# A decoder layer on one core: first and last stage cut by sequence

## The reference, cut to what matters

```python
x = x + self_attn(layernorm(x))          # causal, 16 query heads, 4 key heads of 16, rotary positions
x = x + cross_attn(layernorm(x), ctx)    # 16 heads, an integer mask of 256 x 256, the same for all
x = x + ffn(layernorm(x))                # 256 -> 1024 -> relu -> 256, hidden values and w2 rounded to 8 bits

q = rope((h @ Wqa @ Wqb).reshape(b, s, 16, 16))     # low-rank queries
kv = (h @ Wkva @ Wkvb).reshape(b, s, 4, 16, 2)      # low-rank keys and values; k = rope(kv[..., 0])
```

## Time and profile before

| | us |
|---|---|
| median of 3 runs | 1891.46 (1891.41 to 1894.48) |
| the profiled execution | 1879.75 |
| its span | 1878.1 |
| busy in the span: PE | 1683.7 (90%) |
| DVE | 1242.5 (66%) |
| ACT | 1110.7 (59%) |
| POOL | 701.0 (37%) |

### The profile page before, as it was taken

How to read it: one execution, slowest core, us unless ns; L and a number is a source line. 1 busy time by engine, 2 the same in 40 slices (tenths; PEclk the granted TensorE clock), 3 DMA queues, 4 the chain that set the end, 5 groups by cost and what they waited for, 6 DMA issues and landing times.

```text
span 1878.1 us, 34264 instructions
## 1 busy us (share of the span) xinstructions
PE 1683.7 (90%) x12302; PEld 1017.6 (54%) x12302; DVE 1242.5 (66%) x1908; ACT 1110.7 (59%) x1720; POOL 701.0 (37%) x962
## 2 busy tenths in 40 slices
PE   2879989899998989999899999989999898999887
PEld 1445555556554655655556554655655555565554
DVE  4467576676857667575776857668585766857562
ACT  3355665756567465656756566475656746565563
POOL 3260533625144261533526153262524426152300
PEclk7879999999999999999999998999999999999999
DMA  6351632725254270633626163271625427063310
GB/s 173 51 89 26 94 66 37 121 26 86 47 80 78 35 124 8 87 64 52 106 35 94 31 93 65 35 124 20 89 50 74 84 35 111 18 88 55 51 31 12
DMA packets 86607, 124.09 MB, mean 66 GB/s; under 512 B 10481, under 2 KB 53938, under 8 KB 86322
## 3 DMA queue, kind: packets, MB, share of 16 engines
q1 hardware_dynamic: 83650, 115.26, 40.5%
q0 software_dynamic: 2160, 7.87, 1.1%
q10 hardware_dynamic: 768, 0.57, 0.1%
HBM read 21.42 MB, written 8.39 MB: 16 GB/s over the span
## 4 chain that ended last, share of the span: by engine, by line
PE 62%; POOL 9%; issue 9%; ACT 7%; DMA 7%; DVE 6%; SPq 1%; POOLq 0%; ACTq 0%
PE o_pair L1312 12%; PE small L1398 7%; PE score L1273 6%; PE small L1429 5%; PE small L1143 4%; DMA Q<-q2p 3%; PE small L1325 3%; DVE negmax L894 3%; PE score L1250 3%; DMA Q<-negT 2%; PE score L1231 2%; PE score L1196 2%; PE small L1159 2%; POOL x L494 2%; POOL q1f L518 2%
## 5 line engine op out<-in xcount | busy, mean ns | idle before, releaser
L689 ACT ACTIVATE P<-score 128x1024 f32<-128x1024 f32 x448 | 448.4, 1025 | 145.5 <-PE score L1250 56.6
L894 DVE TENSOR_REDUCE negmax<-score 128x4 f32<-128x1024 f32 (+1 forms) x384 | 463.3, 1221 | 66.4 <-PE score L1231 49.9
L916 DVE TENSOR_TENSOR P<-P,cross_bound 128x1024 f32<-128x1024 f32 x192 | 251.0, 1330 | 118.1 <-ACT P L689 118.1
L1312 PE MATMUL o_pair<-P,V 128*32 128x256 f32 (+1 forms) x4096 | 293.8, 374 | 0.3 <-DVE P L916 0.3
L465 POOL TENSOR_TENSOR negrest<-negmax,negparts 128x32 f32<-128x32 f32 x64 | 15.9, 248 | 629.9 <-ACT negparts L650 629.5
L735 ACT ACTIVATE score<-cross_q 128x1024 f32<-128x1024 bf16 x192 | 194.9, 1021 | 31.8 <-DVE negmax L894 31.1
L1429 PE MATMUL small<-xnT,w 128*128 128x256 f32 x720 | 185.2, 379 | 0.0
L1273 PE MATMUL score<-Q,K 99*128 99x256 bf16 x1024 | 168.1, 291 | 8.2 <-ACT P L689 4.3
L1312 PEld LDWEIGHTS o_pair<-P,V 128*32 128x32 f32 x4096 | 87.3, 109 | 142.7 <-issue 86.7
L1231 PE MATMUL score<-K,Q 96*128 96x256 bf16 x768 | 119.3, 279 | 40.1 <-ACT score L735 19.7
L1273 PEld LDWEIGHTS score<-Q,K 99*128 99x128 bf16 x1024 | 87.4, 102 | 112.4 <-issue 63.6
(11 more groups left out here) (181 smaller groups left out, 3142.1 us busy)
## 6 DMA issues: line engine op xcount, KB each, us to landing
Q<-q1p SPq DMA_DIRECT2D x96, 256.0 KB, 5.9
K<-k2p SPq DMA_DIRECT2D x96, 256.0 KB, 8.3
Q<-q2p SPq DMA_DIRECT2D x192, 128.0 KB, 4.5
x_in<-in_x SPq DMA_DIRECT2D x16, 512.0 KB, 5.6
ctxT<-in_ctx SPq DMA_DIRECT2D x16, 512.0 KB, 6.3
k2f<-q1f SPq DMA_DIRECT2D x32, 256.0 KB, 4.9
out_y<-x POOLq DMA_DIRECT2D x15, 512.0 KB, 6.1
K<-k1p SPq DMA_DIRECT2D x96, 64.0 KB, 4.5
```

What stands on the lines that cost most here:

```text
L689: A.activation(P[:, t % 4, :], score[b][:, :, :], ACT.Exp, scale=SCALE).then_inc(score_free[b], 1)
L894: V.tensor_reduce(negmax[:, k, h:h + 1024 // w], s.rearrange("p (h w) -> p h w", w=w), AX.X, ALU.max, negate=True).then_inc(score_free[b], 1)
L916: V.tensor_tensor(p, p, cross_bound[:, t % 2, :].unsqueeze(1).broadcast_to([128, 4, SEQ]), ALU.min).then_inc(probs_masked[1], 1)
L1312: last = T.matmul(o_ps[ob][32 * j:32 * j + 32, SEQ * gg + q0:SEQ * gg + SEQ], v, p, start=s == 0, stop=end, tile_position=(0, 32 * j), ski ...
```

## The change

The first stage. SP loads the mask, `b2` and `w2` right after the eight small weights and ahead of `ctxT` and the twelve others, each with a semaphore of its own. DVE prepares the mask and rounds `w2` and `b2` ahead of the rotation. The rotation and the cut into parts of the queries go by sequence (256 of the 512 tokens of each of two feature tiles), first sequence first; the keys' rotation, rest and third part move from POOL to DVE, between those of the queries. The query transfers are halved: 2 x 6 of 128 KB, all for the first sequence ahead of those for the second. The six key transfers are issued from POOL's queue. ACT writes the ones of `K2` in two pieces, ahead of its first copy and behind the values, and those of `K1` last. PE starts on the scores of the first sequence when its queries and the keys are there, waits for `loaded` only ahead of `key2`, and waits for the second sequence's queries ahead of tile 6. The transposes of the mask no longer wait for `loaded`.

The end stage. The first sequence's attention output is turned inside `attend`, after tile 15 of the shifted scores and ahead of the last three products with V. `out2_0` comes ahead of the last unit's turn. Residual, norm sums, inverse root, norm, turn (`xnT3_0`, `xnT3_1`), hidden tiles and output go by sequence: `h0_0` to `h0_3` are the hidden tiles of the first sequence (two tiles of 256 tokens to a bank), then `xnT3_1`, `ffn0`, `h1_0` to `h1_3`, `ffn1`. On DVE the last unit's `normalise` stands behind the norm's sums of the first sequence.

```diff
-END_USERS = over(2, ["m2T_1", "o2t0", "o2t1", "o2t2", "oT2_0", "o2t3", "out2_0", "oT2_1", "out2_1", "xnT3_0",
-                     "xnT3_1"] + [f"h{t}" for t in range(HT)] + ["ffn0", "ffn1"])
+END_USERS = over(2, ["m2T_1", "o2t0", "o2t1", "oT2_0", "o2t2", "out2_0", "o2t3", "oT2_1", "xnT3_0", "out2_1"]
+                 + [f"h0_{j}" for j in range(HT // 2)] + ["xnT3_1", "ffn0"] + [f"h1_{j}" for j in range(HT // 2)]
+                 + ["ffn1"])
...
 @block.sync
+            def put_queries(n, b, done):
+                at = slice(SEQ * b, SEQ * b + SEQ)
+                for t, p in enumerate(Q_PART):
+                    if p == n:
+                        sp.dma_start(Q1[HD * t:HD * t + HD, :, at].rearrange("d (h c) t -> d h c t", c=NC),
+                                     q1p[:, n, :, at]).then_inc(done, 16)
...
             sp.wait_ge(loaded_self, 16 * LOADS_SELF)
+            sp.dma_start(mask[:, :, :], d["mask"]).then_inc(loaded_mask, 16)
+            sp.dma_start(b2[:, :], d["b2"]).then_inc(loaded_w2, 16)
+            sp.dma_start(w2[:, :, :], d["w2"]).then_inc(loaded_w2, 16)
             sp.dma_start(ctxT[:, :, :], ctx_v[0]).then_inc(ctx_loaded, 16)
...
             swap_pairs(PRO)
             for n in range(3):
-                put_part("k1", n, 0)
-                put_part("q1", n, 0)
+                sp.wait_ge(first_q1, (4, 6, 7)[n])
+                put_queries(n, 0, stacked_first)
+            for n in range(3):
+                sp.wait_ge((part1, part2, part3)[n]["q1"], 1)
+                put_queries(n, 1, stacked["q1"])
...
 @block.gpsimd
-            rope_products("k1", cosk, sink, k1s, 0)
-            rope_sum("k1", k1s, 0)
-            rest("k1", 0)
-            third("k1", 0)
+            for n in range(3):
+                pool.wait_ge((part1, part2, part3)[n]["k1"], 1)
+                for t, p in enumerate(K_PART):
+                    if p == n:
+                        pool.dma_start(K1[HD * t:HD * t + HD], k1p[:, n, :]).then_inc(stacked_first_k1, 16)
...
-            inverse_root(2, NG - 1)
+            for b in range(GB):
+                pool.wait_ge(ln_step[2], LN_STEPS * (NG + b))
+                at = slice(2 * b, 2 * b + 2)
+                G.tensor_tensor(rstd[2][:, at], vareps[2][:, at], minus_half[:, at], ALU.pow).then_inc(rstd_ready[2], 1)
...
 @block.scalar
             A.activation(carrier[:, 0:1], minus_half[:, 0:1], ACT.Exp)
+            ones(K2[KROWS:SROWS, 0:HEADS // 2, :])
             turns(PRO, "xnT1_", inT)
...
             values1(PRO)
+            ones(K2[KROWS:SROWS, HEADS // 2:HEADS, :])
+            first_part(0)
             part("k1", 0, whole, part1, 0)
-            part("q1", 0, whole, part1, 0)
+            first_part(1)
             part("k1", 1, rest1, part2, 0)
-            part("q1", 1, rest1, part2, 0)
-            for t in (K1, K2):
-                A.activation(t[KROWS:SROWS, :, :], ...)
+            second_part(0)
+            second_part(1)
+            ones(K1[KROWS:SROWS, :, :])
...
+            turn_batch(END, "oT2_1", 1, inT)
+            turn_batch(END, "xnT3_0", 0, xnT3)
+            hidden_half(0)
+            turn_batch(END, "xnT3_1", 1, xnT3)
+            ffn_out(END, 0)
+            hidden_half(1)
+            ffn_out(END, 1)
...
 @block.vector
+            product(q[0], cosq, first_q1)
+            product(other[0], sinq, first_q1)
+            dve.wait_ge(swapped["k1"], 32)
+            product(k, cosk, cosine["k1"])
+            product(other_k, sink, sine["k1"])
+            dve.wait_ge(first_q1, 2)
+            summed(q[0], other[0], first_q1)
+            ...
+            summed(k, other_k, whole["k1"])
+            product(q[1], cosq, cosine["q1"])
+            dve.wait_ge(first_q1, 4)
+            V.tensor_tensor(q[0], q[0], q1p[:, 0, :, 0:SEQ], ALU.subtract).then_inc(first_q1, 1)
+            dve.wait_ge(part1["k1"], 1)
+            V.tensor_tensor(k1f[:, :], k1f[:, :], k1p[:, 0, :], ALU.subtract).then_inc(rest1["k1"], 1)
+            product(other[1], sinq, sine["q1"])
+            dve.wait_ge(first_q1, 6)
+            V.tensor_tensor(q1p[:, 2, :, 0:SEQ], q[0], q1p[:, 1, :, 0:SEQ], ALU.subtract).then_inc(first_q1, 1)
+            dve.wait_ge(part2["k1"], 1)
+            V.tensor_tensor(k1p[:, 2, :], k1f[:, :], k1p[:, 1, :], ALU.subtract).then_inc(part3["k1"], 1)
+            ...
+            summed(q[1], other[1], whole["q1"])
             bk = PRO.bank("maskT")
...
+            normalise(END, 1, 2, NG - 1)
+            for b in range(GB):
+                at = range(2 * b, 2 * b + 2)
+                residual(END, "out2", b, x3, x2)
+                residual_done(END, "out2", b)
+                norm_stats(2, x3, NG - 1 + b, at, at)
+                if b == 0:
+                    normalise(END, 1, 3, NG - 1)
+                norm_apply(2, x3, NG - 1 + b, at)
...
 @block.tensor
                 else:
-                    pe.wait_ge(stacked["q1"], 16 * TERMS * (i + 1))
-                    pe.wait_ge(stacked["k1"], 16 * TERMS * (i + 1))
+                    pe.wait_ge(stacked_first, 16 * TERMS)
+                    pe.wait_ge(stacked_first_k1, 16 * TERMS)
                     self_scores(i, [0, 1])
                 self_scores(i, [2])
                 if not prev:
+                    pe.wait_ge(loaded, 16 * LOADS)
                     pe.wait_ge(ctx_loaded, 16 * (i + 1))
                     key2(st, 0)
...
+                if not prev:
+                    pe.wait_ge(stacked["q1"], 16 * TERMS)
                 self_scores(i, [6])
...
+            batch_copied(END, "oT2_0")
+            tokens(END, "out2", inT, wo2, 0)
+            unit_turn(END, 1, NG - 1, 3)
+            for u in range(2, UNITS):
+                pe.wait_ge(small_free[END.bank(f"o2t{u}")], END.this(f"o2t{u}"))
+            turned_batch(END, "oT2_1", 1, o)
+            pe.wait_ge(xn_ready[2], NG)
+            turned_batch(END, "xnT3_0", 0, xn)
+            batch_copied(END, "oT2_1")
+            tokens(END, "out2", inT, wo2, 1)
+            batch_copied(END, "xnT3_0")
+            hidden_half(0)
+            pe.wait_ge(xn_ready[2], NG + 1)
+            turned_batch(END, "xnT3_1", 1, xn)
+            ffn_ready(0)
+            ffn_out(END, 0)
+            batch_copied(END, "xnT3_1")
+            hidden_half(1)
+            ffn_ready(1)
+            ffn_out(END, 1)
```

More of the change, by code:

```diff
@@ L702, in exponentials @@
                     turn_batch(st, "oT1_0", 0, oT)
+                if last:
+                    turn_batch(st, "oT2_0", 0, inT)
                 unit_out(UNITS - 1)
@@ L838, in _, with hidden_half @@
             cut_first(1, NG - 1, 1)
[L839 to L849, removed]
+            exponentials(END, 1, NG - 1, last=True)
+            def hidden_half(b):
+                for j in range(HT // 2):
+                    bk = END.bank(f"h{b}_{j}")
+                    act.wait_ge(small_full[bk], END.this(f"h{b}_{j}"))
+                    bank, free = small[bk], small_free[bk]
+                    A.activation(carrier[:, j:j + 1], minus_half[:, 0:1], ACT.Copy)
+                    for n in range(2):
+                        t = 2 * j + n
+                        last = A.activation(hq[:, t, SEQ * b:SEQ * b + SEQ], bank[:, SEQ * n:SEQ * n + SEQ], ACT.Relu,
+                                            bias=b1[:, t:t + 1], saturate=False)
+                    last.then_inc(free, 1)
+            turn_batch(END, "oT2_1", 1, inT)
[5 more added lines that the diff above has]
+            ffn_out(END, 1)
         @block.vector
@@ L1378, in attend @@
                         times_v(st, a, g, t - LAG)
+                    if at_end == "last" and t == n:
+                        for u in range(2):
+                            pe.wait_ge(small_free[st.bank(f"o2t{u}")], st.this(f"o2t{u}"))
+                        turned_batch(st, "oT2_0", 0, o)
                     u = (t - LAG - 2) // TPU[a] - 1
@@ L1461, in _ @@
                 value1(PRO, r)
-            pe.wait_ge(loaded, 16 * LOADS)
             bk = PRO.bank("maskT")
@@ L1593, in _ @@
-            pe.wait_ge(small_free[END.bank("oT2_1")], END.this("oT2_1"))
-            tokens(END, "out2", inT, wo2, 1)
-            pe.wait_ge(xn_ready[2], NG)
-            for c in range(NC):
-                turned(END, f"xnT3_{c}", xn, c)
-            copied(END, "xnT3_")
-            hidden(END, range(HT))
-            pe.wait_ge(small_free[END.bank(f"h{HT - 1}")], END.this(f"h{HT - 1}"))
-            for r in range(2):
-                ffn_out(END, r)
+            attend(END, 1, NG - 1, "last")
@@ new lines, in hidden_half @@
+            def hidden_half(b):
+                at = slice(SEQ * b, SEQ * b + SEQ)
+                for j in range(HT // 2):
+                    bk = END.bank(f"h{b}_{j}")
+                    pe.wait_ge(small_free[bk], END.before(f"h{b}_{j}"))
+                    bank, filled = small[bk], small_full[bk]
+                    for n in range(2):
+                        t = 2 * j + n
+                        for c in range(NC):
```

(9 more changed lines are left out.)

93 lines of the change are left out of this document (38 added, 55 removed).

## The result

The changed kernel takes 1873.18 us (median of 8 runs, 1869.71 to 1879.8), the kernel before 1891.02 (8 runs, 1881.7 to 1894.48). The ratio is 0.992, 95% interval 0.9897 to 0.9943: 10.8 to 19.5 us faster. 1876.5 was predicted, with a range of 1867 to 1887. Timed again beside other runs of before, it gave 0.9918 (0.9897 to 0.9938), 15.0 us between the medians.

What follows compares the result with a forecast made beforehand. TensorE bounds the untouched loop; the gain lies where PE stands still at both ends. Start 11 us plus end 4 us give 15: 1891.46 - 15 = 1876.5 us, range 1867 to 1887.

Steps and rivals of the forecast that it cites:

- The swap: First stage: the swapped queries land at 24.5 us as before, since the same bytes are loaded.
- DVE's steps: First stage, rotation on DVE: 0.62 us a step, 1.14 at most; five steps end at 27.65.
- POOL's issues: First stage, six key transfers issued from POOL: 0.86 us each at first, the last ending at 34.1.
- Rival B: First stage: POOL's issues are slow, first score at 44.4, kernel 1882 us; chance 0.09.
- "earliest": First score's early limit: POOL's last issue plus its stores' quickest landing, 34.1 + 3.4 = 37.5 us.
- The rate: First stage transfers: 1.18 MB needed by the first score at 129 GB/s take 9.1 us.
- Behind the first score: Second sequence's queries through at 44.9, tile 6 due at 49.7: covered by 4.8 us.
- The end: End stage by sequence, fewer PE waits: 4 us gained, between 1 and 6.
- "the cost is as before": End stage: if the clock falls behind PE's pause, it costs some 2.8 us as before; gain about 3.
- The difference of 11.7 us: Whole kernel: the median's excess over the profiled time before, carried over unchanged to the forecast.
- "a mean group over 112.5 us": Loop: a mean group time above 112.5 us would show the forecast wrong.
- rival D: Loop falls in otherwise: slow groups more often, 1889 us, or less often, 1866; chance 0.13, of which 0.08 slow.

Runs made afterwards that it cites:

- all queries first: Changed kernel, but the first score also waits for the second sequence's query transfers; 1881.26 us, run once under the profiler.
- small loads first: Changed kernel with the six small or short-rowed of the twelve other weights loaded ahead of the six large ones; 1880.97 us, run once under the profiler.

## Why the prediction was right, step by step

**The swap** was to be unchanged at 24.5. It was 26.05, the late landing just told. That is the 1.5 us by which this profile's gain of 9.15 falls short of 11.0; over the interval the gain is 25.71 - 15.05 = 10.66, and 10.1 to 10.9 in six further profiles of kernels with this start (15.64 with the keys on SP, 14.77 to 15.16 in the others).

**DVE's steps** were taken as 0.62 us. The rows from 26 to 35:

```profile
26.66 0.69 DVE L1038 TENSOR_TENSOR k2f<-k2f,sinq 128x512 f32<-128x512 f32 x1
27.27 0.68 DVE L1038 TENSOR_TENSOR k1f<-k1f,cosk 64x512 f32<-64x512 f32 x1
...
33.29 0.68 DVE L1043 TENSOR_TENSOR q1f<-q1f,k2f 128x512 f32<-128x512 f32 x1
...
34.82 2.87 DVE L1081 TENSOR_TENSOR q1f<-q1f,q1p 128x512 f32<-128x512 f32 x1
38.39 0.69 DVE L1083 TENSOR_TENSOR q1p<-q1f,q1p 128x512 bf16<-128x512 f32 x1 [0.70 <-ACT q1p L805]
```

From start to start it is 0.60 (26.05, 26.66, 27.27), for 64 partitions as for 128. SP's first issue came at 29.84; that is the predicted 28.3 moved by the 1.5 us of the swap. The prediction said that POOL had no arithmetic there any more. It has, and a later paragraph of the prediction names it: its sum of `x_in` (34.38 to 37.13) lies beside the second half's rest, which took 2.87 us instead of 0.68. That step failed, and cost nothing: it is off the path, and it only sets why SP's twelve issues take 10.46 us with gaps, why `x_in` is issued at 40.41 and not 38, and, in the kernel that waits for all the queries, the 2.81 us in the chain above. The Trainium skill, SBUF — State Buffer, "SBUF: two separate sides", says that a VectorE operation with two SBUF inputs and a GpSimd operation that reads SBUF exclude each other on a shared port pair; the trace agrees: 2.87 us beside POOL's 2.75 us, and 0.67 us for the same operation in the kernel with the keys on SP, where POOL was idle.

**POOL's issues** were to cost 0.86 us and end at 34.1. They took 3.26 us for six and ended at 34.38: 0.71 for the first, about 0.5 each for the others, though they begin 2.2 us later, at 31.11 (1.5 from the swap, 0.64 between the semaphore and the issue). Rival B, slow issues, did not come. The last key transfer landed 7.1 us behind its issue, not in the 3.4 us of the prediction's "earliest" case: there was a backlog, as the byte rate wanted it.

**The rate.** 129 GB/s was taken from the kernel before, 141 measured: 1.41 MB in the ten us. A packet of the query halves took 29 ns in the first us (318 packets, 57% of the engines from 31 to 32) and 72 ns with the engines full (528 packets, 118% from 42 to 44), against 66 assumed. The measured first score is 1.8 us later than 39.3 and 1.5 of it are the swap's, so the term of 9.1 us for 1.18 MB came out to some 0.3. In part that is luck, for it had two errors that offset each other: the rate was 9% higher, and 1.41 MB moved ahead of the first score and not 1.18, since 0.23 MB of the second sequence did not wait for the first. The prediction's check on before had the same flaw: the full engines there also carried 0.30 MB of `x_in`.

**Behind the first score.** Tile 6 started at 52.69 with no wait, as said. One small loss wasn't in the sum: the first key matmuls of the next group took 3.05 us instead of 1.9.

```profile
45.11 3.05 PE L1211 MATMUL small<-ctxT,wk 128*128 128x512 f32 x4
...
52.69 0.60 PE L1264 MATMUL score<-K,Q 96*128 96x256 bf16 x4
```

The granted clock was 0.50, 1.2 GHz, in the windows from 21 to 25 and from 40 to 46 us of this execution; in between PE waits 17 us for the queries and keys. In the other kernels that start on the first sequence the same matmuls took 1.88 to 3.16. Counted from DVE's first product, the first store issue came at 230.18 before and at 219.25 in the changed kernel, 10.9 us earlier. Over all profiles it is less: 227.8 to 230.4 in the three with the first stage's order of before, 219.2 to 220.8 in the seven that start on the first sequence, 9.6 us between the means.

**The end** was to give 4 us, from 3 with a fall of the clock to 6 without. It gave 4.3, 4.3 and 4.3 (this profile, the second one, the last stage alone), and in three more with the same end stage tails of 58.8 (keys on SP), 58.6 (all queries first) and 58.0 (small loads first); 0.6 us of the last lie ahead of the last unit's turn. The clock fell in all six, each time behind the pause of 2.39 us, when PE had resumed. The pause was 2.39 us (2.3 said), the waits for ACT 0.68 and 1.07 (0.5 and 1.1). `hidden_half(0)` started at 1848.85 and not 1847.6, since `out2_1` ran at half speed (3.28 us, 1.97 at full speed in the kernel with the last unit normalised first). The windows of the changed kernel, and of before:

```profile
1845.11:1847.11 2.00, 1.85 (x8) 1.58 (x9) 0.10 (x1) 1.12 (x2) 0.00 (x0) 0.79 0.00 0
1847.11:1849.11 2.00, 2.00 (x6) 1.61 (x5) 0.02 (x1) 0.00 (x0) 0.00 (x0) 0.50 0.00 0
1849.11:1851.11 2.00, 2.00 (x9) 1.67 (x9) 1.84 (x7) 0.00 (x0) 0.00 (x0) 0.86 0.00 0
```

The window means 0.79, 0.50 and 0.86 add up to 3.4 us at 0.50; in the kernel before the four windows from 1849.02 on (0.66, 0.50, 0.50, 0.63) give 6.8. The term "the cost is as before", 2.8 us, was too dear: 3.4 us at half speed cost 1.7. That is 1.1 of the 1.3 us by which 4.3 exceeds 3. The forecast of 4 lay between two cases of which neither came as put, so that it came so near is in part luck; the fall came as forecast and only its size was off. (The other bound, 3.2, is an error of the sum: 7.2 less 4.1 and the 0.1 that is left of the displaced 0.4 is 3.0.) By the timed runs the last stage alone is worth 4.6 us, with an interval of 3.2 to 9.8.

**The difference of 11.7 us** between the profiled time of before and the median was carried over, and it held, but the prediction gave no reason for it; only now is it seen where the difference lies. The loop of before's profiled execution, 1560.3 us, is the shortest of eleven. The ten other profiles have 1568.0 to 1576.2 (mean 1571.7), whether the first stage is changed, the last, both or neither. So a typical execution's loop is some 11 us longer than the one in the profile that the sum was made against. Why that one was shorter stays open; its mean granted clock (0.962) is within those of the others (0.953 to 0.966). The prediction's test "a mean group over 112.5 us" wasn't met (112.13), yet rival D would have been misread from the two profiles alone: +9.5 us in the loop looks like a loss that the change made. It isn't: the kernel with halved transfers only, whose loop is that of before, has 1576.2.

**The sum.** 15 us predicted; 15.0 and 17.8 by medians. The two stages gave 13.7 us in the profiles, and 15.2 with the swap's 1.5 us taken out (10.9 and 4.3); by the means over all profiles the start is 9.6 and not 10.9, which gives 13.9. By the means of the runs timed side by side the changed kernel is 15.1 us faster (1889.36 to 1874.24, 8 and 8 runs) and 14.9 us (1887.54 to 1872.64, 11 and 6 runs), each with a standard error of 2 us, so the 17.8 of the first medians is scatter. Nothing has to be looked for in the loop; a gain or loss of 2 or 3 us there isn't excluded.

## What to carry to other kernels

When a stage waits for a backlog of transfers, count the bytes that the first reader needs and split there: the halves cost no more than 4% of the rate (124 against 129 GB/s), and the reader gained 5.9 us of 10.7. Transfers issued behind the ones that are waited for take their share before those have landed: count their bytes too. Small elementwise steps are best on an engine that nobody disturbs (argued from the rows, not tested by itself); look for the other engine's next large operation beside them, also behind the path. A pause that is shortened may only be cut into several: add up all waits behind the edit, and look at the clock, before the gain is put down to it. Do not compare two profiled spans where one execution differs from another by as much as the change: cut both at the same events, and compare stretches that start and end inside one execution.

## What the runs showed of the hardware

- A transfer from SBUF to 16 partitions went at 124 to 141 GB/s over 10 us with all engines full: 129 in runs of 2 KB, 124 in runs of 512 B in the same kernel, 138 and 141 in runs of 512 B from one queue and from two. Transfers of the keys or of the next `x_in` were among them.
- A transfer issue of 64 KB on POOL took 0.71 us the first time and 0.51 in the mean of the five that followed; 512 KB stores take 0.84 to 0.86.
- `w2`'s rounding, 128x2048 to fp8, took 1.23 us with POOL idle and 2.14 us beside POOL's work in the kernel before.
- Between executions of one start, TensorE did the queries' matmuls either in 1.98 us (four, at 17.5) or in 3.77 us, and the swap was issued at 20 or at 22 us. In the second case the record of the granted clock reads 1.00 all through, and the duration is twice as long: near the start of an execution the record and the durations don't agree. That the clock was really at its lower level there is argued from the durations, not shown.
- TensorE's clock fell to 0.50 (1.2 GHz) in the end stage of all six executions with a pause of 2.39 us, and stayed there for 3.4 us; it fell in one of two executions whose pauses were 1.24 and twice 0.78 us, and behind the 4.72 us pause of before it stayed down for 6.8 us.
